# Expert steps of a batch placed behind the next batch's attention, three second halves in front of its first scores

## What is computed

```python
# block 3: attention and feed-forward in hyperbolic coordinates, per batch
q, k, v = _to_heads(plin(xm, w_q, b_q)), ...            # 16 heads of 16
attn = softmax(einsum('bhqd,bhkd->bhqk', qt, kt) / 4)
out_h = expmap0(einsum('bhqk,bhkd->bhqd', attn, vt))
attn_out = plin(_from_heads(out_h), w_o, b_o)
x = mobius_add(residual, expmap0(g_msa * logmap0(attn_out)))
ff = plin(plin(xm, w_f1, b_f1), w_f2, b_f2)             # 256 -> 1024 -> 256
x = mobius_add(residual, expmap0(g_mlp * logmap0(ff)))
# block 4: shared expert and two of four experts, chosen once per batch
gates = softmax(gate_in @ gate_w + gate_b, modulated)   # means over thirds of the tokens
out = x + sw2(gelu(sw1(x))) + sum over top 2 of weight * ew2(gelu(ew1(x)))
```

## Time and profile before

| | us |
|---|---|
| median of 3 runs | 2585.69 |
| lowest, highest | 2585.09, 2587.6 |
| profiled execution, its own time | 2582.36 |
| its span, first to last instruction | 2580.5 |
| TensorE busy | 2359.5 (91%) |
| VectorE, ScalarE, GpSimd busy | 1567.5, 1343.8, 569.9 |
| mean granted TensorE clock | 0.978 |

### The profile page before, as it was taken

The page is one execution under the profiler, slowest core; times in us unless marked ns, Lnnn a source line. Parts: engine busy times, 40 slices in busy tenths (PEclk is TensorE's granted clock), DMA queues, the critical chain, the costliest instruction groups (busy, mean ns, idle before and its releaser), DMA issues.

```text
span 2580.5 us, 96023 instructions
## 1 busy us (share of the span) xinstructions
PE 2359.5 (91%) x39640; PEld 1575.7 (61%) x39640; DVE 1567.5 (61%) x7159; ACT 1343.8 (52%) x4477; POOL 569.9 (22%) x1227
## 2 busy tenths in 40 slices
PE   7899999999999999995557999999999999999998
PEld 6667777777777777774134564655646556465565
DVE  5777777777777777774554664636646356464540
ACT  3555555555555555552644655555565555655532
POOL 0222222222222222222210312203122031220301
PEclk9999999999999999997878999999999999999999
DMA  3111001000000000001101112011110201102020
GB/s 108 42 58 45 27 23 33 27 27 27 24 25 29 26 23 28 26 19 49 41 1 42 70 38 82 1 55 65 50 70 1 86 33 50 70 1 86 10 78 9
DMA packets 45223, 103.11 MB, mean 40 GB/s; under 512 B 9188, under 2 KB 26212, under 8 KB 40052
## 3 DMA queue, kind: packets, MB, share of 16 engines
q1 hardware_dynamic: 41524, 94.45, 10.5%
q10 hardware_dynamic: 3264, 2.52, 0.3%
HBM read 75.93 MB, written 21.04 MB: 38 GB/s over the span
## 4 chain that ended last, share of the span: by engine, by line
PE 35%; DVE 7%; ACT 6%; issue 3%; POOL 2%; DMA 0%; POOLq 0%; ACTq 0%; DVEq 0%
PE bank L788 12%; PE bank L773 11%; ACT pexp L1507 4%; PE bank L956 3%; PE bank L868 2%; PE bank L855 2%; PE bank L948 1%; DVE spl L1236 1%; PE bank L925 1%; PE bank L840 1%; POOL hs L1568 1%; DVE big L1228 1%; DVE uss L1375 1%; PE bank L879 1%; ACT dump L1433 1%
## 5 line engine op out<-in xcount | busy, mean ns | idle before, releaser
L129 PE MATMUL psFI<-wh,Hs 128*8 128x128 f32 (+3 forms) x8192 | 325.5, 276 | 60.3 <-DVE Hs L237 46.5
L129 PE MATMUL psOR<-wh,RH 128*16 128x128 f32 (+3 forms) x8320 | 321.9, 272 | 7.7 <-DMA Hs<-in_condP 3.3
L129 PEld LDWEIGHTS psFI<-wh,Hs 128*8 128x8 f32 (+3 forms) x8192 | 182.5, 99 | 178.8 <-DVE Hs L237 177.8
L1507 ACT ACTIVATE pexp<-bank 128x1024 f32<-128x1024 f32 x256 | 242.0, 1022 | 39.1 <-PE bank L855 39.0
L305 ACT ACTIVATE RH<-RT 128x16 f32<-128x16 f32 x512 | 110.9, 217 | 261.1 <-DVE RT L241 261.1
L788 PE MATMUL bank<-ew,hidden 128*128 128x256 f32 x1024 | 242.4, 380 | 0.0
L773 PE MATMUL bank<-x3T,ew 128*128 128x512 f32 x512 | 241.1, 596 | 0.5
L788 PEld LDWEIGHTS bank<-ew,hidden 128*128 128x128 f32 x1024 | 192.3, 190 | 72.7 <-issue 51.0
L221 DVE STREAM_TRANSPOSE FIT<-psFI 128x128 f32<-128x128 f32 x512 | 162.3, 317 | 120.8 <-PE psFI L129 119.8
L296 ACT ACTIVATE sFI<-FIT 128x32 f32<-128x32 f32 x512 | 118.6, 232 | 210.1 <-DVE FIT L221 206.2
L129 PEld LDWEIGHTS psOR<-wh,RH 128*16 128x16 f32 (+1 forms) x8320 | 206.3, 104 | 10.4 <-issue 6.3
(11 more groups left out here) (272 smaller groups left out, 4497.3 us busy)
## 6 DMA issues: line engine op xcount, KB each, us to landing
ew<-in_ew SPq DMA_DIRECT2D x32, 1024.0 KB, 9.2
qkv_scratch<-qkvr SPq DMA_DIRECT2D x32, 384.0 KB, 2.7
big<-qkv_scratch SPq DMA_DIRECT2D x8, 1536.0 KB, 7.7
XX<-in_xT SPq DMA_DIRECT2D x32, 256.0 KB, 2.8
x_scratch<-xr SPq DMA_DIRECT2D x32, 128.5 KB, 2.4
x<-x_scratch SPq DMA_DIRECT2D x8, 514.0 KB, 8.8
ada<-ada_scratch SPq DMA_DIRECT2D x8, 512.0 KB, 8.3
out_x<-x SPq DMA_DIRECT2D x8, 512.0 KB, 3.3
```

Source lines behind the costliest of these rows:

```text
L129: last = pe.matmul(bank[32 * j:32 * j + width, :], state(k), weights[:, k, j, cols], start=False, stop=k == KC - 1, tile_position=(0, 32 * ...
L1507: up(act.activation(M.pexp[:, n % 2, 2 * pr:2 * pr + 2, :], M.PS[pr][:, :, :], ACT.Exp, scale=1.0 / math.sqrt(HD)), "exps")
```

## The change

`up` and `down` keep their work. What changes is their order and the buffers between them:

- All 24 steps of a batch come behind the next batch's attention, the last three downs (21, 22, 23) one round later, in front of the first scores. `hidden` has five buffers instead of three, and a down follows its up by three steps; the first down of an expert comes one step later still, together with the second.
- Both sets of split transposes of batch b+1 stand at the end of round b, in front of step 21 and of step 23. Their moves stand behind `x_out` on VectorE, and behind `outputs(1)`, `hidden(20)` and `hidden(22)` on ScalarE.
- The results of the shared expert and of the first chosen one go through ScalarE and GpSimd. Those of the last one are added to `x3` by VectorE straight from PSUM (`last_outputs`), in the next round before the gate's logits; SP's store waits for that.
- The gate's logits stand in unit 4, its factors in unit 9, `l_exp` behind unit 6. VectorE makes the choice behind `oT_moved(0)`, and the token weights, the copy of `x3` and the biases behind `oT_moved(1)`.
- VectorE takes two head sums before the first `u_ss` and makes the head factors one chunk earlier, as ScalarE does the roots. GpSimd's third norm power stands before the adds.

The diff, without the parts that only add an argument `batch` to `split_transposes` and `splT_moved`:

```diff
...
 STEPS = (1 + TOPK) * FC
-AFTER_FF, IN_NEXT = FC + 12, STEPS - 2
+LEAD, HIDDEN, IN_NEXT = 3, 5, STEPS - 3
+SPLIT_ACT, SPLIT_DVE = [(0, 0), (0, 2), (1, 0)], [(0, 1), (0, 3), (1, 1), (1, 2), (1, 3)]
...
         self.exp_scratch = sb("exp_scratch", [P, 1])
-        self.hidden, self.weighted = sb("hidden", [P, 3, T]), sb("weighted", [P, NQ, D])
+        self.hidden, self.weighted = sb("hidden", [P, HIDDEN, T]), sb("weighted", [P, NQ, D])
         self.eb2, self.eb1 = [sb(f"eb2_{i}", [P, D]) for i in range(TOPK)], sb("eb1s", [P, TOPK, FC])
...
             pe.wait_ge(*at("x3T_lo", e))
-        elif front and i in (FC, FC + 1):
-            pe.wait_ge(*at("oT", b, i - FC + 3))
+        if i < 2 and front:
+            pe.wait_ge(*at("oT", b, i + 3))
         if i >= 2:
...
         pe.wait_ge(*at("hidden", e, i + 1))
-        if i == 0 and e:
-            pe.wait_ge(*at("y_act", e - 1))
-        elif i == FC:
-            pe.wait_ge(*at("O" if front else "y_dve", b if front else e))
-        elif i == 2 * FC:
-            pe.wait_ge(*at("y_act", e, NQ))
+        if i == 0 and front:
+            pe.wait_ge(*at("O", b))
+        elif i == 0:
+            pe.wait_ge(*at("x3_out", e - 1))
+        elif m == 0:
+            pe.wait_ge(*at("y_act", e, n * NQ))
         if n and m == 0:
...
         for q in range(NQ):
-            last = pe.matmul(M.y_bank(q), M.hidden[:, i % 3, q * P:(q + 1) * P], M.expert(n)[1][:, m, :],
+            last = pe.matmul(M.y_bank(q), M.hidden[:, i % HIDDEN, q * P:(q + 1) * P], M.expert(n)[1][:, m, :],
                              start=m == 0 and q % 2 == 0, stop=m == FC - 1, skip_group_check=True)
...
-        if not experts:
-            return
         for i in range(lo, hi):
             up(i)
-            if i - 2 >= (FC if i >= FC else 0):
-                down(i - 2)
+            if i % FC == LEAD + 1:
+                down(i - LEAD - 1)
+            if i >= LEAD and i % FC != LEAD:
+                down(i - LEAD)
...
             if experts:
-                pe.wait_ge(*at("hidden", e, FC))
+                pe.wait_ge(*at("x3T_lo", e))
+                pe.wait_ge(*at("x3T_hi", e))
         if kc == 0 and g >= 2:
...
+    if b == 0:
+        split_transposes(0, 0)
+        split_transposes(1, 0)
+    if experts:
+        if e:
+            pe.wait_ge(*at("hidden", e - 1))
+        transposes(M.x1, (4, 5), "x3T_ps", "x_out", e)
     if front:
-        split_transposes(0)
-    if e >= 1:
-        down(IN_NEXT, e - 1)
-        pe.wait_ge(*at("hidden", e - 1))
-    if experts:
-        transposes(M.x1, (4, 5), "x3T_ps", "x_out", e)
-    if e >= 1:
-        down(IN_NEXT + 1, e - 1)
-    if front:
-        steps(0, 3)
-        split_transposes(1)
-        steps(3, FC)
-        if experts:
-            down(FC - 2)
-            down(FC - 1)
+        if e >= 1:
+            for i in range(IN_NEXT, STEPS):
+                down(i, e - 1)
         scores(0)
...
             elif experts:
-                up(FC)
-            if n == 1 and experts:
-                pe.wait_ge(*at("y_dve", e))
+                up(0)
+            if n == 4 and experts:
+                if e:
+                    pe.wait_ge(*at("x3_out", e - 1))
                 gate_logits(7)
-            if n == 7 and experts:
+            if n == 9 and experts:
                 gate_factors(7)
...
         if experts:
-            up(FC + 1)
-            down(FC)
-            up(FC + 2)
+            up(1)
+            up(2)
+            down(0)
+            up(3)
         output_transposes(1)
         if experts:
-            down(FC + 1)
+            up(4)
         pe.wait_ge(*at("tT_lo", b))
...
         if experts:
-            up(FC + 3)
-        steps(FC + 4, AFTER_FF)
+            down(1)
+            steps(LEAD + 2, FC + LEAD + 2)
+            up(FC + LEAD + 2)
         transposes(M.z, (0, 1), "zsT_ps", "zs", b)
-    elif experts:
+        if experts:
+            down(FC + 2)
+    else:
+        for i in range(IN_NEXT, STEPS):
+            down(i, e - 1)
         steps(0, 2)
...
         gate_factors(0)
-        steps(5, FC)
-        down(FC - 2)
-        down(FC - 1)
-        steps(FC, AFTER_FF)
+        steps(5, STEPS)
+        for i in range(IN_NEXT, STEPS):
+            down(i)
...
                 second(m - 1)
+        if experts:
+            up(FC + LEAD + 3)
         second(FC - 1).then_inc(M.sem("ff_ps"), 1)
+        if experts:
+            down(FC + 3)
         pe.wait_ge(*at("u_ss", b))
...
         last.then_inc(M.sem("utot_ps"), 1)
-    steps(AFTER_FF, STEPS)
-    if experts and not front:
-        down(IN_NEXT)
-        down(IN_NEXT + 1)
+        if experts:
+            steps(FC + LEAD + 4, STEPS - 3)
+        if b + 1 < NB:
+            split_transposes(0, b + 1)
+        if experts:
+            steps(STEPS - 3, STEPS - 1)
+        if b + 1 < NB:
+            split_transposes(1, b + 1)
+        if experts:
+            steps(STEPS - 1, STEPS)
...
-    def shared_outputs():
...
-        dve.wait_ge(*at("edown", e, FC))
-        if e:
-            dve.wait_ge(*at("y", e - 1))
-        for q in range(NQ):
-            up(dve.tensor_copy(M.weighted[:, q, :], M.y_bank(q)), "y_dve")
+    def last_outputs(e):
...
+        dve.wait_ge(*at("y", e))
+        dve.wait_ge(*at("edown", e))
+        for q in range(NQ):
+            up(dve.scalar_tensor_tensor(M.x3[:, q, :], M.y_bank(q), M.wm[:, 1, q:q + 1], M.x3[:, q, :], ALU.mult, ALU.add), "x3_out")
...
             low_parts(0, q)
-    if front:
-        splT_moved(0, 1)
+        for a, hp2 in SPLIT_DVE:
+            splT_moved(0, a, hp2)
     if experts:
...
         up(dve.tensor_copy(M.x3T[:, 1, :], bank(5)), "x3T_hi")
-    if front:
-        splT_moved(0, 3)
-    if experts:
         gate_input()
-    if front:
-        for hp2 in (1, 2, 3):
-            splT_moved(1, hp2)
+        if e:
+            last_outputs(e - 1)
     if experts and front:
-        shared_outputs()
         gate_logits(7)
-        move_x3()
-        gate_choice()
     elif experts:
...
         expert_biases()
-        shared_outputs()
+        last_outputs(e)
     if front:
...
         if experts:
-            token_weights(7)
-        oT_moved(1)
+            gate_choice()
         o_moved(0)
         o_squares(0)
+        oT_moved(1)
         if experts:
+            token_weights(7)
+            move_x3()
             expert_biases()
...
         heads = b + 1 < NB
+        if heads:
+            head_sums(b + 1, 0)
+            head_sums(b + 1, 1)
         for m in range(1, FC):
...
             up(dve.tensor_tensor(M.uss, M.usq[:, 0, :] if m == 1 else M.uss, M.usq[:, m, :], ALU.add), "u_ss")
-            if heads and m in (1, 2):
-                head_sums(b + 1, 2 * m - 2)
-                head_sums(b + 1, 2 * m - 1)
-                if m == 2:
-                    head_totals(b + 1)
-            if heads and m == 4:
+            if heads and m == 1:
+                head_sums(b + 1, 2)
+                head_sums(b + 1, 3)
+                head_totals(b + 1)
+            if heads and m == 3:
                 head_factors(b + 1)
+            if heads and m >= 4:
+                scaled(b + 1, m - 4)
             if heads and m >= 5:
                 low_parts(b + 1, m - 5)
-            if heads and m >= 4:
-                scaled(b + 1, m - 4)
         if heads:
...
             up(dve.tensor_tensor(M.x1[:, q, :], M.x1[:, q, :], M.x[b % 2][:, q, :], ALU.add), "x_out")
+        if heads:
+            for a, hp2 in SPLIT_DVE:
+                splT_moved(b + 1, a, hp2)
...
             act.wait_ge(*at("eup", e, i + 1))
-            if i >= 3:
-                act.wait_ge(*at("edown", e, i - 2))
+            if i >= HIDDEN:
+                act.wait_ge(*at("edown", e, i - HIDDEN + 1))
             if i == FC:
                 act.wait_ge(*at("eb_in", e))
-            up(act.activation(M.hidden[:, i % 3, :], bank(4 + i % 2), ACT.Gelu_apprx_tanh, bias=M.expert(n)[2][:, m:m + 1]), "hidden")
...
-    def outputs(n, e=e):
...
-        if e < 0:
+            up(act.activation(M.hidden[:, i % HIDDEN, :], bank(4 + i % 2), ACT.Gelu_apprx_tanh, bias=M.expert(n)[2][:, m:m + 1]), "hidden")
...
+    def outputs(n):
...
+        if not experts:
             return
         act.wait_ge(*at("edown", e, (n + 1) * FC))
-        act.wait_ge(*at("y", e, n * NQ))
-        for q in range(NQ):
-            up(act.activation(M.weighted[:, q, :], M.y_bank(q), ACT.Identity, scale=M.wm[:, n - 1, q:q + 1]), "y_act")
+        if n or e:
+            act.wait_ge(*(at("y", e, NQ) if n else at("y", e - 1)))
+        for q in range(NQ):
+            up(act.activation(M.weighted[:, q, :], M.y_bank(q), ACT.Identity, scale=M.wm[:, 0, q:q + 1] if n else 1.0), "y_act")
...
             high_parts(0, q)
+        for a, hp2 in SPLIT_ACT:
+            splT_moved(0, a, hp2)
     if front:
-        splT_moved(0, 0)
-        splT_moved(0, 2)
+        act.activation(M.exp_scratch[:, :], M.mhalf[:, 0:1], ACT.Exp)
     if experts:
...
```

(91 more changed lines are left out.)

8 lines of the change are left out of this document (4 added, 4 removed).

## The result

| | before | changed |
|---|---|---|
| median of the runs, us | 2585.39 (4 runs) | 2548.07 (4 runs: 2546.17 to 2549.76) |
| ratio, 95% interval | | 0.9856 [0.9839, 0.9873] |
| span of the profiled execution | 2580.5 | 2545.5 |
| from scores(0) to scores(0) of the next round, rounds 2 to 6 | 159.42 | 154.71 |
| attention, from its first scores to its last | 30.64 | 30.33 |

The direction was right, and so was the mechanism in the main: waits of TensorE were closed by moving expert halves in front of them. The size was not, and one of the three gaps had two covers where the prediction saw one (e1, e5).

The account below looks back on a forecast made before the run. Rounds 1 to 7 were taken as bound by TensorE's order of work; gains of 14.5 (rounds 2 to 6), 1.8, 2.0, 1.9 and 1.6 sum to 21.8 us, so 2585.7 falls to 2563.9, range 2558 to 2576.

Parts of the forecast that it names:

- gap before the output transposes: TensorE's idle before the second output transposes in a steady round, closed by four halves in front: gain 1.10 us.
- gap before the feed-forward: TensorE's idle before the first feed-forward product, covered by down(10) behind the zs transposes: gain 0.87 us a round.
- gap before the last second half: TensorE's idle before the feed-forward's last second half, covered by up(14) in front: gain 1.13 us a round.
- the gate's place: Inside attention, logits moved from unit 1 to 4 and factors from 7 to 9: loss of 0.2 us a round.
- round 0 to its `x_out`: Round 0, without experts and bound by VectorE at its end: earlier head factors win 2.0 us.
- `x_out` to attention of round 1, without the 16 halves: Start of round 1: about 6 us before attention instead of 7.5, winning 1.5 us.
- slow clock in round 1's attention: Slow clock falls on round 1's first two or three attention units: costs 2 to 4 us, taken as 2.5.
- round 7 and the end, without the 16 halves: Round 7 gains 1.8 us (first two gaps less the gate); the tail behind the last down gains 1.6.
- The rival on the slower side: Round 1's attention stays at 1.2 GHz: 24 us more, kernel 2585, over 2590 with a further drop; chance 0.06.
- The first rival: Later biases bring back a 1.1 us wait at the second output transposes: kernel 2572 to 2576; chance 0.14.
- The second (the gaps only move): Closer-knit order and ScalarE's order make new waits of 3 us a round: kernel 2583 to 2588; chance 0.08.
- the 0.23: TensorE's 0.23 us gap in attention before the last back transposes, forecast to stay in either order.

Follow-up runs that it names:

- e1: Changed kernel with up(14) behind the last second half of the feed-forward instead of in front, early heads kept: round 154.71 us, ratio to before 0.9859.
- e5: Changed kernel with head sums, roots, factors and scaling in the order of the kernel before: round 154.72 us, ratio to before 0.9871.
- e3: Changed kernel with up(3) behind the second output transposes, so three halves before them: round 156.03 us, ratio to before 0.9900.
- e2: Changed kernel with down(10) in front of the zs transposes instead of behind them: round 155.82 us, ratio to before 0.9888.
- e5b: Changed kernel with late heads and up(14) behind the last second half, both undone: round 156.11 us, ratio to before 0.9907.
- e6: Changed kernel with each chosen expert's first down three steps behind its up, like all others: round 155.24 us, ratio to before 0.9869.
- b2: Kernel before with only the early head work (sums before the first u_ss, roots, factors, scaling one chunk earlier): round 157.67 us, ratio 0.9952.
- e4: Changed kernel with gate logits in unit 1, factors in unit 7, l_exp behind unit 3: round 155.02 us, ratio to before 0.9863.
- b1: Kernel before with only up(20) moved in front of the last second half of the feed-forward: round 159.42 us, ratio 1.0004.
- e7: Changed kernel with scores(0) between down(22) and down(23) instead of behind down(23): round 153.62 us, ratio to before 0.9836.
- e9: Changed kernel with down(23) cut in two, two products behind scores(0), two between the pairs of scores(1): round 153.55 us, ratio to before 0.9837.

## Why the prediction was right in direction and wrong in size

A steady round, by the terms of the sum, in us:

| term | forecast | measured, and where |
|---|---|---|
| gap before the output transposes | 1.10 | 1.32, e3 |
| gap before the feed-forward | 0.87 | 1.11, e2 |
| gap before the last second half | 1.13 | 1.40, e5b |
| waits that print no idle | not counted | 0.57: 0.15 and 0.25 in the rows above, restarts 0.07 and 0.10; e6 puts back 0.23 of it at `down(16)`, b2 takes 0.35 away at `up(22)` |
| the gate's place | -0.2 | +0.31, e4 |
| sum | 2.9 | 4.71, as the rounds say |

The whole kernel, by the spans of two single executions. Sixteen halves, 27.5 us, have gone from the third stretch to the last; they are taken out of both:

| stretch | forecast | measured |
|---|---|---|
| first block, to scores(0) of round 0 | 0 | 0.4 |
| round 0 to its `x_out` | 2.0 | 1.5 |
| `x_out` to attention of round 1, without the 16 halves | 1.5 | 1.0 |
| slow clock in round 1's attention | -2.5 | -0.2 |
| rounds 1 to 6, from scores(0) to scores(0), at full clock | 17.4 | 28.3 |
| round 7 and the end, without the 16 halves | 3.4 | 4.1 |
| sum | 21.8 | 35.1, against 35.0 by the spans |

**The step that failed** is the one that priced a gap by the idle time beside its row ("The work is only moved, so the gain is the gap, 1.10", and 0.87, 1.13 in the same way). It mis-sized three right terms by 0.73 us a round in all (3.83 measured against 3.10), and since a short wait prints nothing (the one of 0.25 did not), it left 0.57 more out. That is 1.30 of the 1.81 us a round that were missed, 7.8 over six rounds.

For the gap in the feed-forward the cover was also mis-told: the prediction gives the 1.13 to `up(14)` and nothing to the earlier head sums, which close it alone (e1).

**The gate's sign** was the second: I took the start-up idle in unit 1 for room. It is 0.51 a round between forecast and measurement, 3.1 over six rounds.

**The clock** was the third, 2.3 us. Round 1's attention ran at a granted clock of 0.99 and took 30.55 us against 30.33. The rest of the second split set and the `x3T` transposes, in front of it, had been the slow microseconds:

```profile
1370.00:1376.40 6.40, 5.34 (x40) 4.83 (x40) 4.69 (x9) 3.73 (x6) 0.00 (x0) 0.50 0.29 85
1376.40:1377.00 0.60, 0.60 (x5) 0.13 (x4) 0.44 (x1) 0.53 (x1) 0.00 (x0) 0.50 0.00 0
1377.00:1378.00 1.00, 0.31 (x4) 0.00 (x0) 0.90 (x3) 0.90 (x1) 0.00 (x0) 1.00 0.00 0
```

The clock was at its lower level, 1.2 GHz, until some 0.6 us into the scores, which start at 1376.45, and at 2.4 GHz from there. "Over two or three units that costs 2 to 4" had no row of such a start behind it. The rival on the slower side fell with it. The Trainium skill's rule that I set against the change ("TensorE: Matmul & The Clock Gate", Part 1) did little harm here: the clock fell behind round 0 as it says (0.58 from 1358 to 1370, where TensorE was busy 2.0 of 12 us), and came back early enough to leave 0.22 us of loss.

**What held**: `down(10)` and `up(3)` cover their waits; `x_out` comes long before it is wanted, at 1968.5 against its transposes at 1989.4, 20.9 us later (17 forecast: I had counted 17 halves behind the last second half, and there are 19); the later biases cost nothing; the end won 1.6. Round 0 won 2.8 outside its attention, 2.5 of it by the head work, and its attention gave 1.3 back in that one execution. The first rival (a new wait at the output transposes) did not come: VectorE's `oT(3)` still waits for TensorE, as the prediction said,

```profile
1875.48 0.69 DVE L1255 COPY spl<-bank 128x512 f32<-128x512 f32 x1 [0.73 <-PE bank L869]
```

0.73 us where it waited 0.89. The second (the gaps only move) is true of one part alone, b1, and not of the change, in whose steady rounds only the 0.23 and the waits inside attention are left. One reading was wrong without harm to the sum: that round 7 before is 3.6 us shorter for two sets of split transposes. From scores(0) to the row sums behind the feed-forward it took 107.35 us against 108.75, which is the missing gap of 1.40, and from there to `x_out` 14.72 against 16.93, with no next heads beside it.

What each part gives can't be read off by adding undone parts: `up(14)` and the early heads are each worth 0 in a steady round of the changed kernel, and 1.40 together.

## What to carry to other kernels

On an engine whose instruction ends are modelled, price a wait by the distance from start to start against that of an undisturbed pair, and look for waits that print no idle: here 3.1 us of printed gaps were 4.4 us of time, unprinted waits included. Move cover in front of all chains of a round at once, since one half moved alone only opened the next wait (b1). And look for an order on the waiting engines first: two head sums and one chunk earlier on VectorE and ScalarE made the kernel before 12 us faster without touching the bound engine (b2).

## What was not expected of the hardware

- Attention of round 0, the same program in all runs, took 30.0, 31.1, 31.3 or 32.3 us from its first scores to its last. The granted clock over it was 1.00, 0.95 and 0.89 in windows of three of these executions: the longer, the lower. What lowers it is open. The one of 0.89 is e3:

```profile
1250.90:1283.30 32.40, 28.73 (x188) 6.19 (x188) 6.93 (x18) 28.26 (x30) 5.11 (x2) 0.89 0.08 29
```

- A change of product form costs TensorE 0.21 us there and back, with no idle printed: e7's whole down between two groups of scores and e9's two pieces each take that much more. Within a down the trace's instructions start every 0.216 us; in each piece of e9 the second starts 0.32 behind the first, and the scores start 0.31 behind the last. The last step is no wait for ScalarE: scores(0), which waits for no exponential of its round, also starts 0.31 behind the down in front of it. The two forms differ in type (fp16, fp32) and in the rows of the array (64, 128); which of the two it is was not tried.
- The slow first instruction is not only there behind a wait. The `up` behind the eight small row sums takes 1.96 (b2) with none:

```profile
1987.59 0.95 PE L963 MATMUL bank<-ones_,uss 128*128 128x1 f32 x8
1988.40 1.96 PE L773 MATMUL bank<-x3T,ew 128*128 128x512 f32 x4
```
